# A fused decoder layer whose engines follow written-out step lists: every list laid out anew

## The chip, the core and the metric

The kernel runs on one core of a Trainium2 chip. Its five instruction queues are named as in the profile: PE (TensorE, matrix products), DVE (VectorE), ACT (ScalarE), POOL (GpSimd) and SP (SyncE, which here only issues the transfers). Each queue runs its instructions strictly in the order in which they are written and talks to the others through semaphores. The metric is the device time of one execution in microseconds (us).

## What is computed

One decoder layer over x of shape (8, 256, 512): a linear attention with a memory, a gated long convolution (32 heads of 8 rows each, along the 512 columns), and a feed-forward block with 4-bit weights. Each is followed by a residual sum and a layer norm.

```python
x = layernorm(x + attn(x, w_q, w_k, w_v, w_o, gate, M, z))
#   attn: sq, sk = elu(q)+1, elu(k)+1; memory = sq@M/(sq@z); local = causal sums of sk,v; mix by sigmoid(gate); @ w_o
x = layernorm(x + conv(ctx, ctx, x, ssm_kernel, D, head_dim=8))
#   kv = k_i * v_j per head; y = causal convolution of kv with ssm_kernel (+ D on lag 0); out_j = sum_i y_ij * q_i
x = layernorm(x + ffn(x))
#   gate, up = x @ dequant(gate_up).T; h = silu(gate)*up; y = h @ dequant(down).T; y / rms(y)
```

## The kernel before

The work has two parts. The **first stage** prepares weights and runs the attention of all tokens in eight slots (i = 0 to 7). The **bodies** then run eight groups of 256 rows. Body g computes the convolution of group g and, one group behind, the feed-forward block of group f = g - 1. Body 1 is mixed into the end of the first stage (its steps carry a "+" in the START lists). Body 2 is written out, bodies 3 to 6 are a hardware loop, body 7 is written out without the work that would prepare a ninth group, and body 8 (the LAST lists) holds only the feed-forward block of the last group.

What sets the order on each engine is a list of step names, written by hand into `decoder_layer`: START_SYNC, START_PE, START_DVE, START_ACT and START_POOL for the first stage and body 1, PE_ORDER, DVE_ORDER, ACT_ORDER and POOL_ORDER for a body, and the LAST lists. The helper `run` walks each list. A step is a fixed handful of instructions with its own waits. No scheduler comes after that.

The steps of a body that the text below names:

- PE: `g{i}_{p}` is one quarter (p = 0 to 3) of the gate-and-up product of hidden tile i (0 to 10), four products of 256 columns (L1284, L1286) into one of three PSUM banks (i modulo 3). `y0_{i}` and `y1_{i}` are the down product of tile i for row half 0 or 1, three products of 512 columns (L1297 to L1299). y1 runs a body late. `c{u}` is convolution unit u (0 to 15), three products of 288 columns for each of u%4+1 blocks (L137 to L139), `d0`, `d1` are c0, c1 of the next group. `ct`, `rt`, `xt` are four transposes each (L102).
- ACT: `rs{i}_{p}` rescales bank i between two quarters (two instructions, L1134). `gu{i}` is the silu (L1141), `hh{i}` rounds the hidden tile to 16 bits (L1151), `hk{h}` and `kn` round the key-value products (L180), `n0`, `n1` square the output rows (L1162). `rv`, `ct`, `xt`, `ho` are copies.
- DVE: `gu{i}` multiplies gate and up (L1201), `tm{u}` multiplies convolution unit u with the queries (five instructions, L239 to L257), `lk{h}` and `ln` make the low half of the key-value products (L216), `a`, `b`, `e` finish the output rows (L1207 to L1232), `bs`, `bn`, `nm` the norm behind the convolution, `kq` turns the queries.
- POOL: `pr{h}` and `pn` make the key-value products (four instructions, L197 to L208), `tr{h}` adds up the terms of four units (L297, L299, L304), `hl{i}` makes the low half of hidden tile i (L1102), `a`, `b`, `bn` are roots of a single column (L1098, L308).

The waits that matter: `g{i}_{p}` waits for `rs{i}_{p}`. `g{i}_0` waits for the DVE's `gu{i-3}`, and g0_0 also for both `xt` steps of the body before. `c{u}` waits for `tm{u-2}`, and from one h = u//4 to the next for `lk`. DVE `gu{i}` waits for ACT `gu{i}` and for `hh{i-2}` and `hl{i-2}`, since the tile buffer `h32` has two places. `pr{h}` waits for the `lk` before it, `hk{h}` for `pr{h}`, `lk{h}` for `hk{h}`. `tr{h}` waits for `tm{4h+3}`. `rt1` waits for `tr3`. `y0_{i}` and `y1_{i}` wait for `hl{i}`.

In the first stage the names are: Q and V (projections of a slot), X (its transposes), S, M, N, T, O (scores, memory, local sums, transposed output, out projection), `nm{i}` on ACT (the normalized rows of slot i), and on SP `x{i}` (load of slot i into a ring of five buffers), `st{i}` (its nine stores: rows once, blocks of 64 KB eight times), `xq`, `xr`, `cx`, `toe` (loads for the convolution) and `tw` (the split kernel to memory). `xq0` waits until the blocks of slots 0 to 3 have landed.

## Time and profile before

| | us |
|---|---|
| median of 3 runs | 537.16 |
| lowest and highest | 536.99, 537.49 |
| the profiled execution: its span | 535.3 |
| PE busy in it | 508.7 (95%) |
| ACT, POOL, DVE busy in it | 415.7, 394.7, 374.4 |
| DMA queue, share of 16 engines | 29.6% |

The span runs from the first to the last instruction that the profiler saw. The timed figure lies 1.9 us above it. In the profile a product that follows another overlaps it, because its end is modelled. How long a product really holds PE is therefore read from the distance of two starts. An engine's step is written here as name@time, with the time from the start of the body on PE, that is from the first product of y1_0.

### The profile page before, as it was taken

The numbers are of one execution on the slowest core, as the hardware profiler recorded it, in microseconds if no ns is written. First come the engines' busy times: TensorE is split into PE (matmuls) and PEld (weight loads), VectorE is DVE, ScalarE is ACT, GpSimd is POOL, SyncE is SP. The second block draws the span as 40 slices with busy tenths as digits, with TensorE's granted clock in tenths as the row PEclk, the third lists the DMA queues.
The fourth block names the chain that finished last, engine by engine and source line by source line (L and its number), as shares of the span: only waits on it lengthen the run. The fifth ranks groups of instructions, "written<-read, shape, count | busy, mean of one in ns | idle before, by whom it ended". The sixth has DMA issues, their size and how long they took to land.

```text
span 535.3 us, 11768 instructions
## 1 busy us (share of the span) xinstructions
PE 508.7 (95%) x3676; PEld 377.6 (71%) x3676; DVE 374.4 (70%) x1145; ACT 415.7 (78%) x994; POOL 394.7 (74%) x449
## 2 busy tenths in 40 slices
...
GB/s 224 203 39 63 169 142 180 128 80 99 87 112 24 159 127 86 23 100 79 60 1 117 59 59 0 118 59 59 13 130 14 39 33 49 0 1 42 1 21 39
DMA packets 66146, 40.63 MB, mean 76 GB/s; under 512 B 37882, under 2 KB 55418, under 8 KB 66106
## 3 DMA queue, kind: packets, MB, share of 16 engines
q1 hardware_dynamic: 66106, 40.13, 29.6%
...
q14 instruction: 20, 0.16, 0.1%
...
## 4 chain that ended last, share of the span: by engine, by line
PE 36%; POOL 27%; issue 19%; ACT 5%; DVE 4%; SPq 4%; DMA 2%; POOLq 1%; DVEq 0%; ACTq 0%
POOL shared L297 9%; POOL h_lo L1102 5%; SPq L415 4%; POOL kv L197 3%; PE p_cv L137 3%; PE p_cv L139 3%; PE p_cv L138 3%; PE p_n L1299 3%; PE p_n L1297 3%; PE p_n L1298 3%; POOL shared L299 2%; PE p_x L1284 2%; PE p_x L1286 2%; PE p_qk L1284 2%; PE p_qk L1286 2%
## 5 line engine op out<-in xcount | busy, mean ns | idle before, releaser
L1102 POOL TENSOR_TENSOR h_lo<-w,h_hi 128x256 f16<-128x256 f32 x88 | 73.6, 842 | 44.6 <-ACT h_hi L1151 43.0
L137 PE MATMUL p_cv<-kv_hi,toe 128*128 128x288 f16 x320 | 91.6, 286 | 1.3 <-DVE shared L257 1.3
L139 PE MATMUL p_cv<-kv_hi,toe 128*128 128x288 f16 x320 | 91.5, 286 | 0.0
L138 PE MATMUL p_cv<-kv_lo,toe 128*128 128x288 f16 x320 | 91.5, 286 | 0.0
L1134 ACT ACTIVATE p_qk<-p_qk,rescale 128x256 f32<-128x256 f32 x192 | 78.3, 451 | 12.5 <-PE p_qk L1286 11.9
L297 POOL TENSOR_TENSOR shared<-shared 128x1024 f32<-128x1024 f32 x32 | 76.8, 2399 | 8.9 <-DVE shared L257 8.8
L1134 ACT ACTIVATE p_x<-p_x,rescale 128x256 f32<-128x256 f32 x192 | 78.4, 452 | 6.2 <-PE p_x L1286 6.0
L1134 ACT ACTIVATE p_s<-p_s,rescale 128x256 f32<-128x256 f32 x144 | 59.0, 456 | 11.2 <-PE p_s L1286 11.1
L1297 PE MATMUL p_n<-wd_hi,h_hi 128*128 128x512 f16 x176 | 66.8, 379 | 0.0
L1298 PE MATMUL p_n<-wd_lo,h_hi 128*128 128x512 f16 x176 | 66.7, 379 | 0.0
L1299 PE MATMUL p_n<-wd_hi,h_lo 128*128 128x512 f16 x176 | 66.7, 379 | 0.0
L1284 PE MATMUL p_qk<-x_hi,wg_hi 128*128 128x256 f16 x256 | 63.0, 273 | 3.6 <-DVE x_lo L285 2.1
L1284 PE MATMUL p_x<-x_hi,wg_hi 128*128 128x256 f16 x256 | 62.9, 273 | 0.7 <-ACT p_x L1134 0.2
L1286 PE MATMUL p_x<-x_lo,wg_hi 128*128 128x256 f16 x256 | 62.8, 273 | 0.0
L1286 PE MATMUL p_qk<-x_lo,wg_hi 128*128 128x256 f16 x256 | 62.8, 273 | 0.0
L239 DVE TENSOR_TENSOR shared<-p_cv,qv 128x128 f32<-128x128 f32 x128 | 36.1, 282 | 32.4 <-PE p_cv L139 31.8
L216 DVE TENSOR_TENSOR kv_lo<-kv,kv_hi 128x1152 f16<-128x1152 f32 x32 | 52.6, 1642 | 3.4 <-ACT kv_hi L180 3.4
L242 DVE TENSOR_TENSOR shared<-p_cv,qv 128x128 f32<-128x128 f32 x128 | 49.7, 388 | 0.0
L299 POOL TENSOR_TENSOR shared<-shared 128x512 f32<-128x512 f32 x32 | 47.7, 1492 | 2.5
L1284 PE MATMUL p_s<-x_hi,wg_hi 128*128 128x256 f16 x192 | 47.1, 273 | 0.9 <-ACT p_s L1134 0.9
L1286 PE MATMUL p_s<-x_lo,wg_hi 128*128 128x256 f16 x192 | 47.1, 273 | 0.0
L180 ACT CAST kv_hi<-kv 128x1152 f16<-128x1152 f32 x32 | 37.3, 1166 | 10.9 <-POOL kv L208 7.2
...
## 6 DMA issues: line engine op xcount, KB each, us to landing
...
```

The costliest lines, as they stand in the source:

```text
L137: nc.tensor.matmul(dst, hi, kh, start=(mb == 0), stop=False)
L138: nc.tensor.matmul(dst, hi, kl, start=False, stop=False)
L139: done = nc.tensor.matmul(dst, lo, kh, start=False, stop=(mb == lb))
L297: nc.gpsimd.tensor_tensor(T[:, :, 0:256], T[:, :, 0:256], T[:, :, 256:512], ALU.add).then_inc(cv.tree, 1)
L299: nc.gpsimd.tensor_tensor(T[:, :, 0:128], T[:, :, 0:128], T[:, :, 128:256], ALU.add).then_inc(cv.tree, 1)
L1102: nc.gpsimd.tensor_tensor(h_lo[:, i, :], h32[:, i % 2, :], h_hi[:, i, :], ALU.subtract).then_inc(h_low, 1)
L1134: done = nc.scalar.activation(sums, sums, ACT.Copy, scale=rescale[:, p - 1, part * GI + i:part * GI + i + 1])
L1284: nc.tensor.matmul(dst, whi, cv.x2_hi[:, k, :], start=(k == 0 and part == 0), stop=False, skip_group_check=True)
L1286: done = nc.tensor.matmul(dst, whi, cv.x2_lo[:, k, :], start=False, stop=True, skip_group_check=True)
L1297: nc.tensor.matmul(p_y[t][:], h_hi[:, i, c], wd_hi[:, i, :], start=(i == 0), stop=False)
L1298: nc.tensor.matmul(p_y[t][:], h_hi[:, i, c], wd_lo[:, i, :], start=False, stop=False)
L1299: done = nc.tensor.matmul(p_y[t][:], h_lo[:, i, c], wd_hi[:, i, :], start=False, stop=(i == GI - 1))
```

## The change

Every list is replaced by another permutation of the same steps. Within each body (first stage with body 1, full body, last body) the set of steps on each engine is the same as before. Two waits are added: `deviations` waits for the semaphore that its own engine raised in the slot before, and `add_residual` waits for `fin_made` of the group before, which its own engine raised, too.

```diff
         def deviations(i):
             act.wait_ge(mean_made, i + 1)
+            wait(act, deviated, 2 * i)
...
         def add_residual(f, t):
             dve.wait_ge(rr_made[t], f + 1)
             dve.wait_ge(cv.x2_held[t], f + 1)
+            wait(dve, fin_made[t], f)
...
-    START_SYNC = ("x3 x4 cx2 st0 cx3 tw0 x5 st1 st2 x6 st3 toe0 xq0 xq2 toe1 xq1 x7 cx5 cx4 xr1 xr0 toe2 st4 cx6 xq3 "
+    START_SYNC = ("cx2 tw0 toe0 x3 cx3 x4 st0 x5 st1 x6 st2 st3 xq0 xq1 x7 xq2 toe1 cx4 xr0 cx5 xq4 toe2 cx6 "
...
-    PE_ORDER = ("y1_0 g0_0 g1_0 y1_1 g0_1 y1_2 ct0 g1_1 g0_2 y1_3 y1_4 g2_0 g0_3 c2 g1_2 g3_0 c3 y1_5 g2_1 g1_3 g3_1 "
+    PE_ORDER = ("y1_0 y1_1 g0_0 g1_0 g2_0 y1_2 y1_3 g0_1 g1_1 y1_4 g2_1 g0_2 y1_5 g1_2 ct0 g2_2 c2 c3 c4 "
+                "g0_3 g1_3 g2_3 c5 g3_0 g4_0 y1_6 y1_7 g3_1 g4_1 g5_0 y1_8 g3_2 c6 c7 c8 g5_1 g4_2 y1_9 g3_3 "
+                "c9 c10 g4_3 g5_2 y1_10 g6_0 g7_0 g5_3 c11 g6_1 g8_0 g7_1 c12 c13 g6_2 g7_2 c14 c15 ct1 g6_3 "
...
-    DVE_ORDER = ("tm0 tm1 gu0 lk1 tm2 tm3 gu1 tm4 tm5 gu2 lk2 tm6 tm7 tm8 gu3 tm9 tm10 lk3 tm11 gu4 a1 tm12 gu5 tm13 "
+    DVE_ORDER = ("tm0 tm1 lk1 tm2 tm3 gu0 gu1 gu2 tm4 lk2 tm5 tm6 tm7 tm8 tm9 gu3 gu4 lk3 gu5 tm10 tm11 a1 "
...
-    POOL_ORDER = ("pr1 hl0 pr2 tr0 hl1 pr3 tr1 hl2 hl3 pn a1 hl4 hl5 tr2 tr3 hl6 bn0 b1 hl7 bn1 hl8 hl9 hl10 a0 b0").split()
+    POOL_ORDER = ("pr1 pr2 hl0 hl1 tr0 pr3 hl2 tr1 hl3 pn tr2 hl4 hl5 a1 tr3 b1 bn0 hl6 bn1 hl7 hl8 hl9 hl10 "
+                  "a0 b0").split()
...
-    LAST_DVE = ("gu0 gu1 gu2 a1 gu3 gu4 gu5 b1 gu6 gu7 gu8 e1 gu9 gu10 A1 B1 a0 b0 E1 e0").split()
+    LAST_DVE = "gu0 gu1 gu2 gu3 gu4 a1 b1 gu5 gu6 gu7 gu8 gu9 gu10 e1 A1 B1 a0 E1 b0 e0".split()
```

**POOL, in a body, from the end of pr3 on** (rows of body 7, which has no pn; `shared<-shared` in a row of three is one `tr`, `h_lo` is one `hl`). Before:

```order
L208 TENSOR_TENSOR kv32<-kT1 128x128
L297 TENSOR_TENSOR shared<-shared 128x4x256
L299 TENSOR_TENSOR shared<-shared 128x4x128
L304 TENSOR_TENSOR shared<-shared 128x32x8
L1102 TENSOR_TENSOR h_lo<-w32,h_hi 128x256 x2
L1098 TENSOR_TENSOR rr<-ms,halfneg 128x1
L1102 TENSOR_TENSOR h_lo<-w32,h_hi 128x256 x2
L297 TENSOR_TENSOR shared<-shared 128x4x256
```

After:

```order
L208 TENSOR_TENSOR kv32<-kT1 128x128
L1103 TENSOR_TENSOR h_lo<-w32,h_hi 128x256
L297 TENSOR_TENSOR shared<-shared 128x4x256
L299 TENSOR_TENSOR shared<-shared 128x4x128
L304 TENSOR_TENSOR shared<-shared 128x32x8
L1103 TENSOR_TENSOR h_lo<-w32,h_hi 128x256
L297 TENSOR_TENSOR shared<-shared 128x4x256
```

hl2 moved ahead of tr1, and hl1 (not in these rows) ahead of tr0; hl3 stays right behind tr1, and in a full body pn and tr2 follow it, with hl4 and hl5 behind tr2 and not ahead of it.

**DVE, in a body, around lk3** (rows of body 2; `kv_lo1<-kv32,kv_hi1` is lk3, `w32<-` is a `gu`, a run of five `shared<-p_cv` is a `tm`). Before:

```order
L216 TENSOR_TENSOR kv_lo1<-kv32,kv_hi1 128x1152
L239 TENSOR_TENSOR shared<-p_cv1,qv1 128x32x4
L242 TENSOR_TENSOR shared<-p_cv1,qv1 128x4x8x4
L248 TENSOR_TENSOR shared<-p_cv1,qv1 128x32x2
L251 TENSOR_TENSOR shared<-p_cv1,qv1 128x2x16x2
L257 TENSOR_TENSOR shared<-p_cv1,qv1 128x2x2x32
L1201 SCALAR_TENSOR_TENSOR w32<-p_x,c_up,w32 128x256
L1207 TENSOR_SCALAR ms<-ss 128x1
```

After:

```order
L1202 SCALAR_TENSOR_TENSOR w32<-p_qk,c_up,w32 128x256
L1202 SCALAR_TENSOR_TENSOR w32<-p_x,c_up,w32 128x256
L216 TENSOR_TENSOR kv_lo1<-kv32,kv_hi1 128x1152
L1202 SCALAR_TENSOR_TENSOR w32<-p_s,c_up,w32 128x256
L239 TENSOR_TENSOR shared<-p_cv0,qv1 128x32x4
L242 TENSOR_TENSOR shared<-p_cv0,qv1 128x4x8x4
L248 TENSOR_TENSOR shared<-p_cv0,qv1 128x32x2
L251 TENSOR_TENSOR shared<-p_cv0,qv1 128x2x16x2
L257 TENSOR_TENSOR shared<-p_cv0,qv1 128x2x2x32
```

Before, tm10 stood ahead of lk3 and tm11, gu4 behind it; now gu3, gu4, lk3 and gu5 stand in a row, and tm10 and tm11 come behind gu5.

**SP, in the first stage, after the first fifteen loads.** Before:

```order
L406 DMA z<-in_x 128x2x512
L406 DMA fin<-in_x 128x2x512
L419 DMA cnat<-in_ctx 128x1x512
L410 DMA x_rows<-ring 128x2x512
L415 DMA x_blocks<-ring 8x64x32 x8
L419 DMA cnat<-in_ctx 128x1x512
L462 DMA toeplitz_rows<-kpad 32x1280
L406 DMA ring<-in_x 128x2x512
L410 DMA x_rows<-ring 128x2x512
L415 DMA x_blocks<-ring 8x64x32 x8
```

After:

```order
L419 DMA cnat<-in_ctx 128x1x512
L462 DMA toeplitz_rows<-kpad 32x1280
L423 DMA toe<-toeplitz_rows 128x4x512
L406 DMA z<-in_x 128x2x512
L419 DMA cnat<-in_ctx 128x1x512
L406 DMA fin<-in_x 128x2x512
L410 DMA x_rows<-ring 128x2x512
L415 DMA x_blocks<-ring 8x64x32 x8
L406 DMA ring<-in_x 128x2x512
L410 DMA x_rows<-ring 128x2x512
```

The load of slot 5 (`ring<-in_x`) now stands directly behind the stores of slot 0, whose buffer it reuses; the loads of slots 3 and 4 (`z`, `fin`) stand behind three other transfers.

## Rows read from the trace of the kernel before

**Rows 1.** Busy time by stretch: bounds, length, PE, PEld, DVE, ACT, POOL (instructions), PE clock, DMA.

```profile
1.28:127.30 126.02, 115.16 (x744) 92.41 (x744) 92.86 (x266) 79.22 (x163) 88.76 (x119) 1.00 0.59 140
...
176.10:226.93 50.83, 50.83 (x388) 37.90 (x386) 37.51 (x120) 42.20 (x105) 43.05 (x45) 1.00 0.44 97
...
278.14:329.34 51.20, 51.02 (x387) 37.71 (x386) 38.47 (x121) 42.89 (x106) 42.90 (x45) 1.00 0.22 61
431.74:481.92 50.18, 49.57 (x370) 35.65 (x369) 35.17 (x118) 39.92 (x101) 39.70 (x41) 1.00 0.08 22
481.92:525.20 43.28, 41.91 (x276) 26.07 (x274) 12.45 (x28) 36.18 (x98) 10.08 (x16) 1.00 0.07 19
```

**Rows 2.** Timeline of PE around a body's start: start, duration, line, operands [idle before].

```profile
329.12 0.38 PE L1299 MATMUL p_n<-wd_hi,h_lo 128*128 128x512 f16 x1
329.34 0.38 PE L1297 MATMUL p_n<-wd_hi,h_hi 128*128 128x512 f16 x1
...
330.33 0.28 PE L1284 MATMUL p_qk<-x_hi,wg_hi 128*128 128x256 f16 x1 [0.18 <-DVE x_lo L285]
330.45 0.27 PE L1286 MATMUL p_qk<-x_lo,wg_hi 128*128 128x256 f16 x1
330.56 0.27 PE L1284 MATMUL p_qk<-x_hi,wg_hi 128*128 128x256 f16 x1
...
336.43 0.30 PE L137 MATMUL p_cv<-kv_hi,toe 128*128 128x288 f16 x1
336.56 0.29 PE L138 MATMUL p_cv<-kv_lo,toe 128*128 128x288 f16 x1
```

**Rows 3.** Timeline of POOL, tr0 to hl2 of the body that starts at 278.14.

```profile
291.59 2.37 POOL L297 TENSOR_TENSOR shared<-shared 128x1024 f32<-128x1024 f32 x1
...
295.48 1.64 POOL L304 TENSOR_TENSOR shared<-shared 128x256 f32<-128x256 f32 x1 [0.16 <-POOL shared L299]
297.08 0.67 POOL L1102 TENSOR_TENSOR h_lo<-w,h_hi 128x256 f16<-128x256 f32 x1
297.71 1.27 POOL L197 TENSOR_TENSOR kv<-kT 128x512 f32<-128x512 f32 x1
...
300.44 2.36 POOL L297 TENSOR_TENSOR shared<-shared 128x1024 f32<-128x1024 f32 x1
...
304.92 2.41 POOL L1102 TENSOR_TENSOR h_lo<-w,h_hi 128x256 f16<-128x256 f32 x2
```

**Rows 4.** Timeline of DVE: three of the 32 instructions of L216 (`lk`, `kl`).

```profile
287.00 1.36 DVE L216 TENSOR_TENSOR kv_lo<-kv,kv_hi 128x1152 f16<-128x1152 f32 x1 [0.58 <-ACT kv_hi L180]
...
294.81 1.72 DVE L216 TENSOR_TENSOR kv_lo<-kv,kv_hi 128x1152 f16<-128x1152 f32 x1
...
93.52 2.81 DVE L216 TENSOR_TENSOR kv_lo<-kv,kv_hi 128x1152 f16<-128x1152 f32 x1
```

**Rows 5.** Timeline of POOL and ACT at a body's end: a0, b0, pr1, an rs.

```profile
330.49 0.55 POOL L1098 TENSOR_TENSOR rr<-ms,halfneg 128x1 f32<-128x1 f32 x1 [2.16 <-DVE ms L1207]
...
333.96 1.27 POOL L197 TENSOR_TENSOR kv<-kT 128x512 f32<-128x512 f32 x1
...
330.98 0.81 ACT L1134 ACTIVATE p_qk<-p_qk,rescale 128x256 f32<-128x256 f32 x2 [0.25 <-PE p_qk L1286]
```

**Rows 6.** Costliest groups: counts, busy us, mean ns of one, idle before by releaser.

```profile
L180 ACT CAST kv_hi<-kv 128x1152 f16<-128x1152 f32 x32 | 37.3, 1166 | 10.9 <-POOL kv L208 7.2 <-PE p_cv L139 3.7
...
L1151 ACT CAST h_hi<-w 128x256 f16<-128x256 f32 x88 | 36.1, 411 | 2.2 <-DVE w L1201 1.8
...
L1201 DVE SCALAR_TENSOR_TENSOR w<-p_x,c_up,w 128x256 f32<-128x256 f32 x32 | 15.4, 481 | 14.3 <-ACT w L1141 14.3
```

**Rows 7.** SP's queue in the first stage: the block stores of slot 0, the first `xq` loads.

```profile
38.37 7.19 SPq L415 DMA_DIRECT2D x_blocks<-ring x8
...
83.34 4.90 SPq L426 DMA_DIRECT2D xq<-x_blocks x2
```

**Rows 8.** Timeline of PE at the start of the last body: g0_1 after its wait.

```profile
485.88 0.28 PE L1284 MATMUL p_qk<-x_hi,wg_hi 128*128 128x256 f16 x1 [0.55 <-ACT p_qk L1134]
```

More of the change, by code:

```diff
@@ L1359, in decoder_layer @@
-    START_ACT = ("xa0 kw0 kw1 xb0 kw2 kw3 re0 ge0 vk0 ks0 xa1 xb1 lc0 rv0 wh0 wh1 re1 ok0 kt0 wh2 rv1 wh3 qs0 xa2 vk1 "
[8 rows of a table removed]
-                 "+hh10 nm7 +xt1 +n0").split()
-    START_POOL = ("id0 ms0 ws0 ws1 ws2 ws3 ws4 ws5 pr0 ws6 ws7 pw0 ws8 ws9 ws10 pr1 ws11 ws12 ws13 ws14 ws15 pw1 ws16 "
-                  "pw2 ws17 ws18 ws19 ws20 ws21 ws22 ws23 pw3 ws24 ws25 ws26 ws27 ws28 ws29 ws30 ws31 ws32 pr2 pw4 tr0 "
-                  "pr3 tr1 pr4 tr2 tr3 pq0 +pr1 pq1 +pr2 pw5 +tr0 +hl0 +hl1 pw6 +pr3 +hl2 +tr1 +hl3 +pn +hl4 +tr2 +hl5 "
-                  "+hl6 +tr3 +hl7 +bn0 pw7 +hl8 +bn1 +hl9 +hl10 +a0 +b0").split()
@@ L1374, in decoder_layer @@
-    PE_ORDER = ("y1_0 g0_0 g1_0 y1_1 g0_1 y1_2 ct0 g1_1 g0_2 y1_3 y1_4 g2_0 g0_3 c2 g1_2 g3_0 c3 y1_5 g2_1 g1_3 g3_1 "
[3 rows of a table removed]
-                "y0_8 y0_9 xt1 y0_10").split()
-    DVE_ORDER = ("tm0 tm1 gu0 lk1 tm2 tm3 gu1 tm4 tm5 gu2 lk2 tm6 tm7 tm8 gu3 tm9 tm10 lk3 tm11 gu4 a1 tm12 gu5 tm13 "
-                 "kq0 tm14 tm15 b1 gu6 gu7 ln kq1 bs0 bn0 bs1 bn1 gu8 nm0 gu9 nm1 gu10 xt0 xt1 a0 b0 e1 e0").split()
-    ACT_ORDER = ("rv0 rs0_1 rs1_1 rs0_2 tl rs0_3 rs1_2 gu0 hk1 hh0 rs1_3 rs2_1 rs3_1 rs2_2 gu1 rs3_2 rs2_3 hk2 gu2 hh1 "
-                 "ct0 rs4_1 rv1 rs3_3 rs5_1 rs4_2 rs5_2 gu3 hh2 hk3 rs4_3 rs5_3 rs6_1 n1 hh3 gu4 rs6_2 ho0 gu5 hh4 "
-                 "rs7_1 hh5 kn rs6_3 rs7_2 rs8_1 ct1 rs7_3 rs8_2 gu6 gu7 rs8_3 hh6 rs9_1 rs10_1 rs9_2 ho1 rs10_2 rs9_3 "
-                 "hh7 gu8 rs10_3 gu9 hh8 gu10 hh9 xt0 hh10 xt1 n0").split()
```

39 lines of the change are left out of this document (25 added, 14 removed), and 54 rows, old and new, of tables (LAST_PE, PE_ORDER, START_ACT, START_DVE).

## The prediction

> **What bounds the kernel now.** I read the busy times by stretch first, then the timeline of PE at the stretches' edges, then POOL's and DVE's timelines inside one body. In the body at 176.10 PE is busy for all of its 50.83 us, and in the looped bodies for all but 0.18 of 51.20 [rows 1]. Distances of starts tell what a product really costs: 0.216 us at 512 columns (329.12 to 329.34), 0.11 at 256, 0.12 to 0.13 at 288 [rows 2]. So a `y` takes 0.65 us of PE, a `g` 0.44, a `c` of k blocks 0.37 k, four transposes 0.44. With these a full body holds 50.7 us of PE work: 22 y 14.2, 44 g 19.2, the convolution 14.7, 24 transposes 2.6. The looped bodies give away 0.4 to 0.5 us, nearly all of it in one place: y1_0 starts at 329.34 and would be done at 329.99, but g0_0 starts at 330.33, released by DVE's x_lo [rows 2]. Nothing can be won in a body beyond that half microsecond, and everything can be lost. Slack is elsewhere: the stretch 1.28 to 127.30 has 126.0 us of which PE is busy 115.2, and the last body has waits such as the 0.55 us at g0_1 [rows 1, 8]. POOL is the second bound: busy 42.9 of 51.2 us in a looped body [rows 1], in an order in which each piece waits for DVE or ACT in between.
>
> **What POOL's pieces cost.** A `pr` holds POOL for 2.73 us (297.71 to 300.44), an undisturbed `tr` for 4.48 (300.44 to 304.92). The `tr0` of the same body took 5.49 (291.59 to 297.08), with its L304 at 1.64 us [rows 3], and in that time DVE's lk2 ran, 294.81 to 296.53, in 1.72 us where lk1 took 1.36 [rows 4]. A `kl` that met the 2.37 us instruction L297 took 2.81 [rows 4]. So a `lk` and a POOL step that meet cost POOL about 1.0 us, and the `lk` waits for the end of POOL's instruction. The Trainium skill states this in "SBUF — State Buffer", section "Who interferes with whom": a vector instruction with two SBUF inputs and a GpSimd instruction that reads SBUF exclude one another for the whole instruction. By that rule each meeting would cost POOL up to the whole 1.36 us of the `lk`, where these rows show 1.0.
>
> **The body, walked through in the new order.** PE positions are sums of the step costs above.
> - The tail first. In the loop now the last product of y0_10 ends at 329.50 and pr1 starts at 333.96, 4.5 us later, through n0, a0 (POOL at 330.49), b0 on DVE and b0 on POOL [rows 2, 5]. In the new PE order d1 stands behind y0_10, so y0_10 ends 0.6 us before the next body starts and pr1 starts at 3.9 (now 4.6).
> - pr1 ends at 6.8. ACT must first do rs0_1, rs1_1, rs2_1, rs0_2, rv0, rs1_2, rs2_2 (0.73 us each for a pair [rows 5], 0.5 for rv0), the last fed by g2_1@5.4, so hk1 (1.17 us [rows 6]) runs 7.2 to 8.4, lk1 8.4 to 9.8, pr2 9.9 to 12.6. There is no hl0 in between to fill POOL's 3 us.
> - g0_3 stands behind 6 y, 9 g, ct0, c2, c3 and c4, at 11.2 (now 6.3 by the same count). The three silus and two products behind it (0.48 us each [rows 6]) let hh0 end at 13.6, hl0 runs 13.7 to 14.35, hl1 to 15.0, tr0 starts at 15.0 (now 13.45, as 291.59 less 278.14 [rows 1, 3]).
> - lk2 can start at 16.5 (pr2, then two rs, then hk2), but L297 of tr0 holds until 17.3: lk2 ends at 18.6, tm5 at 19.6. PE stands at c7@18.9, which waits for tm5. **Stall 1: 0.8 us.**
> - tr0 pays the meeting and ends at 20.5, pr3 at 23.2, hl2 at 23.8, tr1 starts. On DVE gu3, gu4 and lk3 stand in a row and gu4 needs g4_3@24.5, so lk3 falls on 26.5 to 28.9, within tr1, which then ends at 29.3; hl3 at 30.0. DVE's gu5 needs hl3 and ends at 30.5. PE has g8_0 behind 11 y, 27 g, ct0 and c2 to c11, at 29.25 plus stall 1, 30.05, and it needs gu5. **Stall 2: 0.6 us.**
> - Behind gu5 DVE has tm10 and tm11, done at 32.2. c13 would start at 31.8 and needs tm11. **Stall 3: 0.5 us.**
> - POOL goes on without a pause: pn to 32.7, tr2 to 37.2, hl4, hl5, a1 to 39.0, tr3 to 43.4. rt1 stands at 41.85 plus 1.9, 43.75: no further stall. gu7 (needs hl5) ends at 39.3, g10_0 stands at 39.4: none.
> - At the end DVE's ln stands behind gu10, at 49.6 to 51.0, and meets hl9. y0_9 stands at 50.2 and needs hl9, which ends at 50.3 without the meeting and 51.1 with it; d0 needs ln. **Stall 4: between 0.1 and 0.9**, taken at 0.3, since which of the two comes first hangs on 0.1 us.
> - In return g0_0 now has y0_8, y0_9, d0, y0_10, d1, y1_0 and y1_1 between it and xt1, and its wait goes.
>
> Sum: 50.7 + 0.8 + 0.6 + 0.5 + 0.3 = 52.9, with 0.1 for handovers 53.0, against 51.2. That is 1.8 us for each of bodies 3 to 6 and 2.1 for body 2: **9.3 us**. The bounds: below, no stall at all, 50.8 and a gain of 0.4 a body; above, stall 4 in full and a second meeting at 1.36, 54.0 and a loss of 2.8.
>
> **Body 7** has no pn, but stalls 1 to 3 stand ahead of it: 48.8 of PE work plus 1.9, 50.7 against 50.18 [rows 1]: **0.5 us**.
>
> **The last body** holds 40.5 us of PE work in 43.3 [rows 1]. The new lists drop ho0 from ACT's start (it goes to the end, behind n0, beside a0 and its root) and ask g0, g1, g2 in turn, in the order in which ACT serves them. Walking it the same way I find waits of 0.2 at g2_2, 0.1 at g3_2, 0.1 at g3_3, 0.2 at g7_2 and some of 0.1, 0.8 in all, so 41.4 where 43.3 stand. Behind the last product, B1's root comes ahead of a0's, and E1 leaves b0's root alone: 0.2 less. Together with 0.2 for the first g0_0, which has three y ahead of it: **minus 2.3 us**, bounds 0 and minus 3.
>
> **The first stage and body 1.** Moved: on SP, the transfer of the kernel and toe0 ahead of x3 and x4, x5 directly behind st0 and x6 behind st1; on ACT nm0 behind qs1, xa3, vk2 and xb3; on DVE u2 and u3 ahead of steps of slots 1 and 2, sk0 and fs0 exchanged. x3 lands at 31 or so and Xa3 needs it at 36: free. nm0 ends at 44 (now 37.9), so st0's nine issues (7.2 us [rows 7]) end at 52, x5 waits 3 us for their landing, x6 likewise, and st3's last block lands 2 us later than now, where xq0 leaves at 83.34 [rows 7]. From there to rt1 POOL runs tr0, pr3, tr1, pr4, tr2, tr3 in both orders, so 2 us come out late. They are given back: pq1 now stands ahead of body 1's pr1 (2.73 us), and c1 and c2 (1.8 us) stand between xt0 and g0_0 as filling. On PE g0_0 has 1.1 us more work ahead of it and comes at 128.7 where it came at 127.3 [rows 1], so 0.3 net. Body 1 is no better or worse by a count that I trust. **Plus 0.4 us**, bounds minus 2 and plus 3.
>
> **The two added waits** ask for what their own engine has finished a slot or a body earlier, nothing is queued by them: 0.
>
> Total: 0.4 + 9.3 + 0.5 - 2.3 = +7.9 us. The profiled span of 535.3 becomes 543.2; the median lies 1.9 above the span, so **545.0 us**.
>
> **The rivals.**
> 1. *The loop runs clean, and the kernel is faster.* Stalls 1 to 3 hang on one run of POOL from 3.9 to 30.0. If it were 1.0 us shorter (lk3 ahead of or behind tr1, or hk1 earlier), gu5 would be done at 29.5 and stalls 2 and 3 vanish; at 1.5 us also stall 1. For it: PE's content is no more than before and the order asks banks in turn. Against it: DVE's gu3, gu4, lk3 in a row put lk3 into tr1. All clean is 5 times minus 0.4, minus 1.5 in body 7 and minus 2.3, with plus 0.4: 532, with small waits left 533. Chance 0.20.
> 2. *Only one stall of the loop is there*, 0.5 to 0.8 a body: 538 to 541. Chance 0.17.
> 3. *More than I count.* Every meeting of a `lk` costs its full 1.36, and stall 4 is full: 0.35 twice and 0.6, 1.2 a body more, 551. By the Trainium skill's page "SBUF — State Buffer" the first half of that is the rule. Chance 0.12.
> 4. *The order does nothing that can be told from no change* (0.2%, about what a measurement of this kernel resolves), by the first stage giving what the loop takes. Chance 0.05.
> The forecast, 541 to 548, keeps 0.46.
>
> **How the numbers follow.** The range reaches from the middle between rivals 1 and 2 to most of rival 3: 535 to 550, leaving 0.15 below and 0.05 above. Faster: rival 1 and a little of the rest, 0.22. Same 0.06, slower 0.72.
>
> **What would show it.** Starts of y1_0 53.0 us apart in the loop (clean: 50.8). Idle PE before c7 (released by L257), g8_0 (by L1202) and c13 (by L257). tr0 and tr1 near 5.5 us both. No idle before g0_0. tr0 at 94.5 to 95 in the first stage. It would be wrong above all if hl3 is done before 29 us into the body, or if PE idles in the loop somewhere that this walk does not name.

## The result, and the profile after

| | before | after |
|---|---|---|
| median (4 runs each) | 537.33 | 548.99 |
| lowest and highest | 536.99, 537.98 | 548.24, 549.54 |
| span of the profiled execution | 535.3 | 547.6 |
| chain that ended last: PE, POOL | 36%, 27% | 23%, 37% |

The change makes the kernel slower: ratio 1.0218, 95% interval 1.0204 to 1.0233. The forecast was 545.0 in a range of 535 to 550. The span grew by 12.3 us. The starts of the bodies (the first product of y1_0, in the last body the first product of its list) say where:

| stretch | forecast | measured |
|---|---|---|
| first stage and body 1 (start of body 2 at 176.10, now 179.14) | +0.4 | +3.0 |
| bodies 2 to 6 (255.6 us, now 267.4) | +9.3 | +11.7 |
| body 7 (50.18, now 50.73) | +0.5 | +0.55 |
| last body to the end of the span (53.4, now 50.3) | -2.3 | -3.0 |

Busy time by stretch, with the columns of [rows 1]. The second line is body 2, the third a looped body, then body 7 and the last body with its tail (43.28 us in [rows 1] leaves the tail out).

```profile
1.28:131.94 130.66, 118.53 (x752) 94.24 (x752) 95.21 (x269) 76.90 (x160) 89.09 (x119) 1.00 0.54 134
179.14:232.53 53.39, 51.75 (x387) 37.45 (x386) 39.55 (x123) 44.69 (x110) 42.10 (x45) 1.00 0.53 124
286.02:339.53 53.51, 51.48 (x388) 37.48 (x386) 38.97 (x121) 42.69 (x107) 41.96 (x45) 1.00 0.20 59
446.52:497.25 50.73, 49.43 (x371) 35.82 (x369) 36.48 (x119) 39.08 (x100) 38.37 (x41) 1.00 0.08 22
497.25:547.59 50.34, 40.92 (x276) 26.13 (x274) 15.08 (x36) 36.67 (x99) 11.91 (x19) 0.95 0.11 27
```

The granted clock is 1.00, the full level of 2.4 GHz, in all of them but the last. There it is 1.00 as well up to PE's last product at 538.3, and 0.72 on average in the 9.3 us behind it, in which PE has nothing to do. PE's busy time includes the ends that the profile models, so 2.03 us of idle in the looped body stand for 2.8 us lost, as the distances of starts give it (50.7 us of work in 53.5).

The timeline of PE in that body, around its four waits (c7, g8_0, c13, d0). Line numbers are one or two higher than in the rows of before: a product of g is L1286 or L1288, y is L1299 to L1301.

```profile
304.80 0.29 PE L139 MATMUL p_cv<-kv_hi,toe 128*128 128x288 f16 x1
305.53 0.30 PE L137 MATMUL p_cv<-kv_hi,toe 128*128 128x288 f16 x1 [0.45 <-DVE shared L257]
...
315.80 0.27 PE L1288 MATMUL p_qk<-x_lo,wg_hi 128*128 128x256 f16 x1
316.78 0.28 PE L1286 MATMUL p_s<-x_hi,wg_hi 128*128 128x256 f16 x1 [0.71 <-DVE w L1202]
...
317.91 0.29 PE L139 MATMUL p_cv<-kv_hi,toe 128*128 128x288 f16 x1
318.51 0.30 PE L137 MATMUL p_cv<-kv_hi,toe 128*128 128x288 f16 x1 [0.31 <-DVE shared L257]
...
336.83 0.38 PE L1301 MATMUL p_n<-wd_hi,h_lo 128*128 128x512 f16 x1
337.77 0.29 PE L137 MATMUL p_cv<-kv_hi,toe 128*128 128x288 f16 x1 [0.56 <-DVE kv_lo L216]
```

Take the distance of the two starts and subtract what the first product holds PE: 0.73 less 0.12 is 0.61 before c7. In the same way 0.87 before g8_0, 0.48 before c13, 0.72 before d0. The idle before g0_0 in [rows 2] is gone. DVE in that body: lk2, then lk3 and what stands behind it, then ln (answers [rows 4], where an undisturbed one took 1.36).

```profile
302.55 2.06 DVE L216 TENSOR_TENSOR kv_lo<-kv,kv_hi 128x1152 f16<-128x1152 f32 x1 [0.62 <-ACT kv_hi L180]
...
312.72 2.18 DVE L216 TENSOR_TENSOR kv_lo<-kv,kv_hi 128x1152 f16<-128x1152 f32 x1
316.24 0.48 DVE L1202 SCALAR_TENSOR_TENSOR w<-p_s,c_up,w 128x256 f32<-128x256 f32 x1 [1.34 <-POOL h_lo L1103]
...
335.74 1.81 DVE L216 TENSOR_TENSOR kv_lo<-kv,kv_hi 128x1152 f16<-128x1152 f32 x1
```

POOL in the same body, tr0, then hl2, tr1 and hl3, then hl9 and hl10 (answers [rows 3]).

```profile
301.03 2.36 POOL L297 TENSOR_TENSOR shared<-shared 128x1024 f32<-128x1024 f32 x1
303.47 2.27 POOL L299 TENSOR_TENSOR shared<-shared 128x512 f32<-128x512 f32 x1
305.90 0.73 POOL L304 TENSOR_TENSOR shared<-shared 128x256 f32<-128x256 f32 x1 [0.16 <-POOL shared L299]
...
309.32 0.68 POOL L1103 TENSOR_TENSOR h_lo<-w,h_hi 128x256 f16<-128x256 f32 x1
309.95 2.38 POOL L297 TENSOR_TENSOR shared<-shared 128x1024 f32<-128x1024 f32 x1
312.41 1.27 POOL L299 TENSOR_TENSOR shared<-shared 128x512 f32<-128x512 f32 x1
313.76 1.72 POOL L304 TENSOR_TENSOR shared<-shared 128x256 f32<-128x256 f32 x1
315.44 0.67 POOL L1103 TENSOR_TENSOR h_lo<-w,h_hi 128x256 f16<-128x256 f32 x1
...
335.66 2.41 POOL L1103 TENSOR_TENSOR h_lo<-w,h_hi 128x256 f16<-128x256 f32 x2 [0.45 <-ACT h_hi L1152]
```

Here the exclusion can be read off. lk2 was issued at 302.55, while L297 ran until 303.39. It ended at 304.61, 1.2 us behind the end of L297. L299 took 2.27 where an undisturbed one takes 1.27, and it ended 1.1 us behind lk2. So first DVE waits for POOL's instruction, then POOL's next one for DVE's. Both pay: lk2 took 0.70 us more than its undisturbed 1.36, L299 1.0 more. tr0 (301.03 to 306.63) and tr1 (309.95 to 315.48) both take 5.5 to 5.6 us. hl3 follows tr1 and ends at 316.11, and DVE's gu5 starts 0.13 us later, DVE having been idle for 1.34 us. g8_0 follows gu5. That is the chain of stall 2.

In the first stage the transfers on SP, as far as the prediction speaks of them (answers [rows 7]): the blocks of slot 0, the first xq, then what was not foreseen, xr2 at 118.23 with xr1 behind it.

```profile
46.02 6.15 SPq L415 DMA_DIRECT2D x_blocks<-ring  x8
...
86.89 0.96 SPq L426 DMA_DIRECT2D xq<-x_blocks  x2
...
118.23 1.35 SPq L430 DMA_DIRECT2D xr<-x_rows  x2
```

And on DVE, bq1 of the first stage, which adds the rows that xr1 loads:

```profile
125.05 0.69 DVE L265 TENSOR_TENSOR shared<-p_ct,xr 128x512 f32<-128x512 f32 x1 [1.98 <-DMA xr<-x_rows]
```

### The profile page after: what moved, and what is told of

Same layout as the page of the kernel before. It is cut to its first block, busy times and chain, and to the rows that moved or that the text cites. A ratio compares the mean times of both kernels' runs of the same rounds, so it can differ in the third digit from the quotient of the medians.

```text
span 547.6 us, 11783 instructions
## 1 busy us (share of the span) xinstructions
PE 512.4 (94%) x3676; PEld 377.4 (69%) x3676; DVE 375.1 (69%) x1145; ACT 413.5 (76%) x994; POOL 388.6 (71%) x449
## 4 chain that ended last, share of the span: by engine, by line
POOL 37%; PE 23%; issue 18%; DVE 11%; ACT 4%; DMA 3%; SPq 3%; POOLq 1%; DVEq 0%; ACTq 0%
POOL shared L297 10%; POOL h_lo L1103 7%; POOL shared L299 4%; POOL kv L197 4%; PE p_n L1299 2%; PE p_n L1301 2%; PE p_n L1300 2%; POOL kv L207 2%; POOL kv L202 2%; SPq L415 2%; POOL shared L304 2%; PE p_qk L1286 2%; PE p_x L1288 2%; PE p_qk L1288 2%; PE p_x L1286 2%
## 5 line engine op out<-in xcount | busy, mean ns | idle before, releaser
L1103 POOL TENSOR_TENSOR h_lo<-w,h_hi 128x256 f16<-128x256 f32 x88 | 65.7, 756 | 38.0 <-ACT h_hi L1152 37.5
L1135 ACT ACTIVATE p_qk<-p_qk,rescale 128x256 f32<-128x256 f32 x192 | 79.7, 466 | 16.0 <-PE p_qk L1288 15.7
L297 POOL TENSOR_TENSOR shared<-shared 128x1024 f32<-128x1024 f32 x32 | 76.7, 2396 | 13.5 <-DVE shared L257 13.5
L1135 ACT ACTIVATE p_x<-p_x,rescale 128x256 f32<-128x256 f32 x192 | 80.1, 473 | 2.5 <-PE p_x L1288 2.5
L1299 PE MATMUL p_n<-wd_hi,h_hi 128*128 128x512 f16 x176 | 66.8, 379 | 0.1
L1301 PE MATMUL p_n<-wd_hi,h_lo 128*128 128x512 f16 x176 | 66.7, 379 | 0.0
L1286 PE MATMUL p_qk<-x_hi,wg_hi 128*128 128x256 f16 x256 | 62.9, 273 | 1.2 <-DVE w L1202 1.0
L216 DVE TENSOR_TENSOR kv_lo<-kv,kv_hi 128x1152 f16<-128x1152 f32 x32 | 56.9, 1779 | 9.2 <-ACT kv_hi L180 9.2
L1286 PE MATMUL p_x<-x_hi,wg_hi 128*128 128x256 f16 x256 | 62.9, 273 | 0.0
L1288 PE MATMUL p_x<-x_lo,wg_hi 128*128 128x256 f16 x256 | 62.8, 273 | 0.0
L1288 PE MATMUL p_qk<-x_lo,wg_hi 128*128 128x256 f16 x256 | 62.8, 273 | 0.0
L197 POOL TENSOR_TENSOR kv<-kT 128x512 f32<-128x512 f32 x32 | 41.1, 1284 | 23.8 <-DVE kv_lo L216 23.7
L1286 PE MATMUL p_s<-x_hi,wg_hi 128*128 128x256 f16 x192 | 47.2, 273 | 4.1 <-DVE w L1202 4.0
L299 POOL TENSOR_TENSOR shared<-shared 128x512 f32<-128x512 f32 x32 | 48.8, 1524 | 2.5
L137 PEld LDWEIGHTS p_cv<-kv_hi,toe 128*128 128x128 f16 x320 | 31.2, 98 | 24.3 <-DVE shared L257 10.2
```

What stands on the lines that cost most here:

```text
L137: nc.tensor.matmul(dst, hi, kh, start=(mb == 0), stop=False)
L297: nc.gpsimd.tensor_tensor(T[:, :, 0:256], T[:, :, 0:256], T[:, :, 256:512], ALU.add).then_inc(cv.tree, 1)
L299: nc.gpsimd.tensor_tensor(T[:, :, 0:128], T[:, :, 0:128], T[:, :, 128:256], ALU.add).then_inc(cv.tree, 1)
L1103: nc.gpsimd.tensor_tensor(h_lo[:, i, :], h32[:, i % 2, :], h_hi[:, i, :], ALU.subtract).then_inc(h_low, 1)
L1135: done = nc.scalar.activation(sums, sums, ACT.Copy, scale=rescale[:, p - 1, part * GI + i:part * GI + i + 1])
L1286: nc.tensor.matmul(dst, whi, cv.x2_hi[:, k, :], start=(k == 0 and part == 0), stop=False, skip_group_check=True)
```

## Experiments

All experiments have the two added waits. "The whole" is the median, a body's length the distance of y1_0's starts in the profiled execution. With the old first stage, the start of body 2 lay between 175.7 and 176.8 in eight kernels that share it, the one before among them, mostly because the wait before c2, behind xq0's landing, varies from 0.5 to 1.3 us. So parts of a microsecond in the whole are read from the bodies, where the looped ones of one kernel agree within 0.04 us.

### One part of the change at a time

**Full body only.**

```diff
 START_*, LAST_*                  (old lists)
-PE_ORDER, DVE_ORDER, ACT_ORDER, POOL_ORDER   (old)
+PE_ORDER, DVE_ORDER, ACT_ORDER, POOL_ORDER   (new)
```

> Only the four full-body lists are the new ones; the first stage, body 1 and the last body keep the old ones (537.3 us as a whole). Theory (the loss is in the body's own cycle: c7 behind tm5, g8_0 behind gu5, c13 behind tm11, d0 behind ln): bodies 2 to 6 cost the 11.7 us that they cost in the changed kernel and body 7 0.6, so 549.5 us, looped body 53.5 us. Rival (the stalls are handed on by the new first stage, whose steps leave POOL and DVE late): with the old first stage the looped body falls back towards 51.2 and the whole to 538 to 543.

Measured 549.67 (ratio 1.0233, 1.0216 to 1.0251). The looped body takes 53.50 and bodies 2 to 6 take 267.38 us, to 0.01 us what they take in the changed kernel. The four waits are the same in place, and in size to 0.01 us. So the loss of the loop is the body's own and nothing is handed on to it.

**First stage and body 1 only.** The new START lists, the other lists old.

> Only the first stage and body 1 are new. Theory (parts add up, the stretch up to body 2 is 3.0 us longer in the changed kernel): 540.3 us. Rival (what the new first stage leaves behind fits only the new body): body 2 also loses 1 to 2 us more, so 541 to 543. Rival (the old body takes the late start up in its own slack): below 539.

Measured 541.41 (1.0080, 1.0063 to 1.0096), so the first rival. Body 2 starts at 178.90, and it takes 52.24 us where it took 50.83. The timeline of ACT and then of PE at the start of body 2:

```profile
179.10 0.60 ACT L1163 ACTIVATE sq<-p_n 128x512 f32<-128x512 f32 x1
179.59 0.19 ACT L1163 ACTIVATION_READ_ACCUMULATOR sq<-p_n 128x1 f32 x1
179.68 1.51 ACT L632 ACTIVATE ring<-ring,shift,rs 128x512 f32<-128x512 f32 x2
181.09 0.60 ACT L174 COPY crev<-cnat 128x512 f32<-128x512 f32 x1
181.60 0.81 ACT L1135 ACTIVATE p_qk<-p_qk,rescale 128x256 f32<-128x256 f32 x2
```

```profile
181.22 0.38 PE L1301 MATMUL p_n<-wd_hi,h_lo 128*128 128x512 f16 x1
182.46 0.28 PE L1286 MATMUL p_qk<-x_hi,wg_hi 128*128 128x256 f16 x1 [0.86 <-ACT p_qk L1135]
```

The new ACT list ends with nm7 (L632, 1.51 us) behind n0. The old body asks rs0_1 for g0_1 behind one y, so g0_1 waits 1.02 us. The new body has y1_2 and y1_3 in between and hides nm7. Here start and body fit one another in the new lists, and testing one alone shows 1.4 us more loss than it causes in the changed kernel.

**Last body only.** The new LAST lists, the others old.

> Only the last body is new. Theory (its own order takes away the 3.1 us in which PE waited between the last bodies' products): 3.0 us less than before, 534.3 us. Rival (the gain came from how the new full body ends, with its hidden tiles and its norm done earlier, not from the last body's list): 536.5 to 537.5 us.

Measured 535.13 (0.9963, 0.9949 to 0.9977). By its own list the last body falls from 53.4 to 50.38 us, as in the changed kernel. But body 7 grows from 50.18 to 51.10, since the new last list begins with g0_0, which comes before the old body's xt1 is through ACT and DVE:

```profile
481.75 0.38 PE L1301 MATMUL p_n<-wd_hi,h_lo 128*128 128x512 f16 x1
482.89 0.28 PE L1286 MATMUL p_qk<-x_hi,wg_hi 128*128 128x256 f16 x1 [0.76 <-DVE x_lo L285]
```

The 3.0 us are the last body's own and 0.9 go at the seam. It is the fastest kernel that still computes everything.

### What makes the waits in the loop

All of these start from the kernel with the new full body only (549.67, looped body 53.50).

**One term step into DVE's idle time.**

```diff
-DVE_ORDER = "... gu3 gu4 lk3 gu5 tm10 tm11 a1 ..."
+DVE_ORDER = "... gu3 gu4 lk3 tm10 gu5 tm11 a1 ..."
```

> The new full body in the old surroundings (looped body 53.5 us, 549.7 as a whole), with one move on DVE: tm10 stands ahead of gu5, where DVE waited 28.88 to 30.23 for hl3, and not behind it. gu5 keeps its time (30.2), tm11 ends 0.8 us earlier, so the 0.48 before c13 goes. Theory A (POOL's run from hl0 to tr3, without a gap from 13.8 to 43.6, is a second bound just behind PE, with rt1 at 43.87 right behind tr3): rt1 now waits 0.2 to 0.4, and the looped body gains 0.1 to 0.3 only, so 548.2 to 549.2. Theory B (each wait of PE counts by itself): the looped body falls by 0.48 to 53.0, the whole by 2.4 to 547.3.

Measured 547.98 (1.0200, 1.0185 to 1.0216), the looped body 53.41. The 0.48 before c13 is gone and gu5 keeps its time (312.52, at 30.22 of the body). But PE now waits 0.19 before g10_0 (for gu7, which waits for hl5) and 0.1 before rt1, and every step of POOL from hl0@13.76 to tr3@43.59 stands where it stood, to 0.03 us. The body gains 0.09, a fifth of the wait that went. That is theory A for the loop. Of the 2.0 us of the span, 0.5 are bodies 2 to 6, 0.5 body 7, where the gain is not taken back (no pn), and 1.0 lies ahead of body 2, in the part that is the same code, so only half of the 2.0 us is an effect of the move.

**ln somewhere else.**

```diff
-DVE_ORDER = "... gu7 b1 bs0 ... gu9 gu10 ln xt1 ..."
+DVE_ORDER = "... gu7 b1 ln bs0 ... gu9 gu10 xt1 ..."
```

> The new full body in the old surroundings (549.7 us), with ln moved on DVE from behind gu10 to behind b1, into the idle 41.2 to 42.7. There it falls into tr3 of POOL (39.05 to 43.57), in place of hl10. Theory A (POOL's tr grows by 1.0 when it meets a low half of the key-value products, as tr0 and tr1 do with 5.5 against 4.5): tr3 ends 0.5 to 1.0 later and rt1 waits as much; hl10 falls from 1.74 to 0.67 and the 0.74 before d0 goes; looped body 53.3 to 53.8, the whole 548.7 to 551. Theory B (the length of tr depends on other things, and only the place of ln counts): rt1 doesn't wait, looped body 52.8, the whole 546.

Measured 550.53 (1.0245, 1.0229 to 1.0261), the looped body 53.67: theory A. The wait before d0 is gone and hl10 falls from 1.74 to 0.68 us. tr3 grows from 4.52 to 5.53, in its L299 as before, and rt1 waits for it by 0.85 us. POOL's tr3 and PE's rt1 behind it:

```profile
322.98 2.35 POOL L297 TENSOR_TENSOR shared<-shared 128x1024 f32<-128x1024 f32 x1
325.41 2.29 POOL L299 TENSOR_TENSOR shared<-shared 128x512 f32<-128x512 f32 x1
327.77 0.73 POOL L304 TENSOR_TENSOR shared<-shared 128x256 f32<-128x256 f32 x1
```

```profile
328.63 0.65 PE L102 MATMUL p_ct<-ident,shared 128*128 128x128 f32 x4 [0.68 <-POOL shared L304]
```

**The low halves cut to a ninth.**

```diff
+        w = slice(0, 9) if isinstance(g, int) and g < 2 else slice(0, 1)
-        nc.vector.tensor_tensor(cv.kv_lo[h % 2][:], cv.kv32[:], cv.kv_hi[h % 2][:], ALU.subtract)
+        nc.vector.tensor_tensor(cv.kv_lo[h % 2][:, w], cv.kv32[:, w], cv.kv_hi[h % 2][:, w], ALU.subtract)
```

> The new full body in the old surroundings (549.7 us); from body 2 on the steps lk and ln make only the first ninth of the low half (128 of 1152 columns), the rest of it keeps older values, so that work is left out. Theory A (the meetings of lk with tr on DVE and POOL carry all four waits): tr0 and tr1 fall from 5.5 to 4.5, hl10 from 1.7 to 0.7, all four waits go, looped body 50.7 to 51.0, the whole 535.5 to 537. Theory B (the order alone makes them: hl3 stands behind tr1, gu5 behind hl3, tm11 behind gu5): only the waits before c7 and d0 go, 0.87 and 0.48 stay, looped body 52.1, the whole 542.5.

Measured 534.16 (0.9941, 0.9926 to 0.9956), 1.3 us below the range of theory A, which left out that body 7 has three of the waits, too (bodies 7 and 8 take 1.9 us less together). All four waits are gone, the looped body takes 50.79 us, which is PE's own work, and PE has 76% of the chain that ended last. tr0 takes 4.61, tr1 4.51, hl10 0.67 us. It does not say yet whether the meetings did it or the time that DVE saved. A looped body of this kernel:

```profile
278.29:329.07 50.78, 50.78 (x388) 37.88 (x386) 34.59 (x121) 42.56 (x107) 38.95 (x45) 1.00 0.22 62
```

**The time kept, the second input taken away.** The same cut, and in its place a reduction over the other 1024 columns, which reads one buffer.

```diff
+            nc.vector.tensor_reduce(cv.spare[:], cv.kv32[:, 1:9]..., axis=X, op=ALU.add)
         nc.vector.tensor_tensor(cv.kv_lo[h % 2][:, w], cv.kv32[:, w], cv.kv_hi[h % 2][:, w], ALU.subtract)
```

> The new full body in the old surroundings (549.7 us, looped body 53.5). From body 2 on lk and ln make only the first ninth of the low half, and a sum over the other 1024 columns of the same buffer (one input from SBUF, its result is never read) fills up their time on DVE to about the 1.36 us of before; so the rest of the low half keeps older values. Theory A (what stretches POOL is that lk reads two inputs from SBUF, as the Trainium skill has it in SBUF - State Buffer, section Who interferes with whom, where a reduction never contends; by the rows alone the same is expected, since DVE's other steps beside a tr leave it at 4.5): tr0, tr1 at 4.5 to 4.6, hl10 at 0.7, no wait before g8_0 and c13, at most 0.1 before c7 and 0.3 before d0, looped body 50.8 to 51.3, the whole 534 to 537. Theory B (the waits come from DVE's 1.4 us at these places, whatever it does in them): tr0 and tr1 at 5.5 or the waits at c7 and d0 as before, looped body 52 or more, the whole above 541.

Measured 541.03 (1.0071, 1.0054 to 1.0088), the looped body 52.05, so neither. tr0 and tr1 are at 4.61 and 4.52 and the waits before g8_0 and c13 are gone, as theory A has it. d0 waits 0.34, as it has it. But c7 waits 0.90 and not 0.1. The two steps of lk2 on DVE, and POOL's tr0 beside them (L304 is here what L297 is elsewhere, L306 is L299):

```profile
296.52 1.22 DVE L221 TENSOR_REDUCE spare<-kv 128x1 f32<-128x1024 f32 x1 [0.62 <-ACT kv_hi L181]
297.65 1.21 DVE L223 TENSOR_TENSOR kv_lo<-kv,kv_hi 128x128 f16<-128x128 f32 x1
```

```profile
295.00 2.37 POOL L304 TENSOR_TENSOR shared<-shared 128x1024 f32<-128x1024 f32 x1
297.45 1.28 POOL L306 TENSOR_TENSOR shared<-shared 128x512 f32<-128x512 f32 x1
```

The reduction ran for 0.85 us beside POOL's L304, and that took its undisturbed 2.37. The little subtraction behind it, with its two inputs, needed 1.21 us for 128 columns (0.43 in lk3 of the same body): it waited until L306 was through at 298.73 and ended at 298.86. So the reduction disturbs nobody, and the remaining two-input piece was shut out for one more POOL instruction, which made lk2 end at 18.9 of the body and not at 18.6. What follows: the waits before g8_0 and c13 come from the two-input meeting, since DVE was almost as busy as before (38.2 us in a looped body, 39.0 without the cut), only with another kind of instruction. The wait before c7 is not separated by this run; in the cut one lk2 ended at 17.53, just behind L297, and c7 did not wait. By the rows of the changed kernel the meeting is enough to explain it: lk2 took 0.70 us longer than undisturbed, and c7 waited 0.61. That is worked out and not shown by a run. Before d0 0.34 of 0.72 us are left without a meeting.

### The first stage

Of these, all four take the new first stage with the old full and last body.

**The order of two loads.**

```diff
-START_SYNC = "... xr0 cx5 xq4 toe2 cx6 xr2 xr1 toe3 ..."
+START_SYNC = "... xr0 cx5 xq4 toe2 cx6 xr1 xr2 toe3 ..."
```

> As the kernel with only the new first stage, but on SP the load xr1 stands ahead of xr2, no longer behind it. xr2 loads group 1's rows into the buffer that bq0 of group 0 empties, so whatever stands behind it is issued only after bq0; in the changed kernel xr1 was issued at 118.23 and bq1 of DVE started at 125.05, behind its landing. Theory (this one place carries 2 of the 3 us of the first stage): bq1 starts about 2 us earlier and the whole is 1.5 to 2.5 us below the kernel with only the new first stage. Rival (the stores and the later norm of slot 0 set it, and bq1's wait is hidden by the next one): within 0.5 us of it.

Measured 539.43 (1.0045, 1.0028 to 1.0062), 2.0 us below the kernel without the swap, and body 2 starts at 176.92 where it started at 178.90. bq1 starts at 122.90, without a wait for rows, and not at 125.05. xr2 waits for bq0 to empty its buffer, and xr1, which had nothing left to wait for, stood behind it.

```profile
122.90 0.68 DVE L265 TENSOR_TENSOR shared<-p_ct,xr 128x512 f32<-128x512 f32 x1
```

**The norms of slots 6 and 7.** nm7 ahead of xt1 of body 1, nm6 behind hh7, pw6 ahead of hl6, nb6 behind gu7, all of body 1; with the swap above.

> The new first stage with xr1 ahead of xr2, old full and last body (539.4 us), and nm6 and nm7 (two squares of slots 6 and 7, 1.5 us each on ACT) moved: nm7 from the very end of ACT's start list, behind n0, to ahead of xt1 of body 1, nm6 from there to behind hh7, with its inputs pw6 and nb6 drawn ahead. Theory (in body 2 rs0_1 stands behind nm7, which ran 177.71 to 179.22, so g0_1 waits 1.03 us; the new full body hid that behind y1_2 and y1_3): body 2 falls from 52.23 to 50.8 to 51.2, the whole to 538.0 to 538.4. Rival (the norms only move the wait into body 1, to g9_0 or xt1, since ACT has no 1.5 us free there): body 1 longer by what body 2 gains, 539.0 to 539.8.

Measured 544.71 (1.0142, 1.0125 to 1.0159). Body 2 takes 51.37, so 0.87 of its 1.4 us were indeed nm7's, but body 1 lost 6 us, far beyond the rival. nm6 now stands ahead of rs8_1, it waits for nb6, that for pw6, and that stands on POOL behind tr3 until 167.25. ACT, and PE's g8_1:

```profile
168.63 1.52 ACT L632 ACTIVATE ring<-ring,shift,rs 128x512 f32<-128x512 f32 x2 [3.53 <-DVE shift L790]
170.06 0.78 ACT L1135 ACTIVATE p_s<-p_s,rescale 128x256 f32<-128x256 f32 x2
```

```profile
170.90 0.28 PE L1286 MATMUL p_s<-x_hi,wg_hi 128*128 128x256 f16 x1 [4.22 <-ACT p_s L1135]
```

**fs0 early.** In addition fs0 on DVE behind dn0.

> As the kernel with the moved norms, and fs0 on DVE (six small instructions on the scales) back behind dn0, where the old list had it near 18 us, from behind o2, where it ran 46.6 to 51.2 because its one-input instructions of 11 and 88 columns took 1.4 to 2.5 us beside POOL's unpacking copies, and where ra2 and rb2 stood behind it (1.46 us wait of PE before V3, st2 and all stores behind it late). Theory A (the delay of slot 2 goes on through nm2 and st2 to xq0 and so to c2): the wait before V3 goes, st2 and xq0 leave 1 to 2 us earlier, the whole falls by 1 to 2 us. Theory B (PE's gain is eaten at c2, whose wait is for xq0, and xq0 hangs on the loads x5 and x6 that stand between the stores): V3's wait goes, c2's wait grows by the same 1.5, within 0.4 us of the kernel with the moved norms.

Measured 546.80 (545.74 to 547.83; 1.0172, 1.0151 to 1.0192). It says nothing on the question: fs0 and sk0 stood in front of o0 and held it from 18.6 to 23.1 us, ACT's ok0 waited 5.05 us, and everything came 3 us later up to body 2.

**fs0 late.** Only the swap of the loads, and fs0 behind o3.

> The new first stage with xr1 ahead of xr2, old full and last body (539.4 us), and fs0 on DVE behind o3, where DVE stood idle from 59.2 to 63.0 us, not behind o2, where it held DVE from 46.0 to 50.6 with ra2 and rb2 queued behind it. (Behind dn0, as in the run before, it waited at 18.6 to 22 in front of o0 and pushed everything 3 us back, which answered nothing.) Theory A (the delay of slot 2 goes on by nm2 and st2, issued at 69.0, to the loads xq0 at 86.25 and kq0 and so to c2): the wait of 1.46 before V3 goes, st2 and xq0 leave 1 to 2 us earlier, the whole comes to 537.4 to 538.4. Theory B (xq0 hangs on the loads x5 and x6 that stand between the stores, x6 issued at 66.09): V3's wait goes, st2 at most 0.5 earlier, c2's wait grows from 2.0 to 3 or more, the whole within 0.4 of 539.4.

Measured 539.68 (1.0050, 1.0033 to 1.0067), no gain over 539.43. fs0 takes 2.1 us there and not 4.5, and V3 starts 0.9 us earlier. But N3 now waits 1.36 us for DVE's AT (0.57 before the move) and starts at 56.66, 0.2 later than without it, and w23 waits another 0.7. st2 and xq0 leave at 69.84 and 87.08, not earlier than their 69.01 and 86.25. The whole is what theory B gave, but not by its way: the gain is gone five microseconds further on, long before xq0 and c2. So the 1.46 us before V3 were no loss that moving fs0 gives back.

### A faster kernel that did not come

The old full body gives away 0.35 us before g0_0, and the new last body 0.9 at the seam.

```diff
-PE_ORDER = "... xt0 y0_7 y0_8 y0_9 xt1 y0_10"
+PE_ORDER = "... xt0 y0_7 y0_8 xt1 y0_9 y0_10"
-LAST_PE = "g0_0 g1_0 g2_0 y1_0 g0_1 ..."
+LAST_PE = "y1_0 g0_0 g1_0 g2_0 g0_1 ..."
```

> The old first stage and full body with the new last body (535.1 us as a whole), and two moves on PE: in the full body xt1 stands one product earlier (ahead of y0_9, its input nm1 was made 1.3 us before it), and in the last body y1_0 stands ahead of g0_0. Theory (g0_0 waits for the last transposed rows by way of ACT and DVE, 0.35 in each looped body and 0.92 at the head of the last body): the looped body falls from 51.20 to 50.85, four or five times 0.35, and 0.9 goes from body 7 to 8, so 532.4 to 533.0. Rival (xt1 runs into the rounding on ACT or the bank and its chain does not move with it, or POOL's run holds rt1): 534 to 535, with a wait at rt1 or at xt1 in place of the one at g0_0.

Measured 537.85 (1.0012, 1.0003 to 1.0021), so the rival, and worse than it. xt1 wants the bank that DVE's x_lo of xt0 drains at 329.25:

```profile
329.40 0.63 PE L102 MATMUL p_ct<-ident,shared 128*128 128x128 f32 x4 [0.43 <-DVE x_lo L285]
```

The wait at g0_0 is gone, xt1 waits 0.59 and c2 0.36, and the looped body takes 51.77 in place of 51.21. At the seam 0.06 us were won: bodies 7 and 8 take 101.42 us together, where with the plain new last body they took 101.48.

## Why the prediction was right, point by point

**Sign and range: right**, but the range held by its width and not by the sum. The span grew by 12.3 us, where the sum had 7.9. At 548.99 the time lies above the 541 to 548 that the prediction called its forecast, 1.0 us below the upper end of a range that was drawn up to 550 for the sake of rival 3. Of the missing 4.4 us, 2.6 lie in the first stage with body 1 and 2.4 in bodies 2 to 6, and the last body gave back 0.7.

**The walk through the body: right in mechanism and place.** All four waits stand where it put them, before c7, g8_0, c13 and d0, with the releasers it named, and no fifth one. Up to tr3 its times held to 0.3 us or better: hl0 forecast 13.7 and measured 13.76, tr0's end 20.5 and 20.6, lk3's 28.9 and 28.88, hl3's 30.0 and 30.09, tr3's 43.4 and 43.57. Stalls 1 to 3 were given 1.9 us and measured 1.96, and here two misses cancel: stall 1 was given 0.8 and measured 0.61, stall 2 0.6 and 0.87, stall 3 0.5 and 0.48.

**Stall 4: under-sized.** The prediction saw a race of ln with hl9 and hl10, between 0.1 and 0.9, and took 0.3, for no better reason than that 0.1 us decides. It measured 0.72. ln was issued at 49.72 of the body, 0.08 us behind the start of hl9. So hl9 was not lengthened (49.64 to 50.31), ln waited for its end, took 1.81 us in place of 1.36 and ended at 51.53 where the walk had 51.0; hl10 behind it took 1.74 in place of 0.67. The walk had left out its own rule, that a `lk` waits for the end of POOL's instruction. Four looped bodies at 2.3 and body 2 at 2.6 are 11.7 us for a forecast of 9.3. This term is most of the difference there.

**The first stage: the step that failed.** Forecast +0.4, measured +3.0. What comes late was seen, but sized too small: st0's issues end at 52.17 (forecast 52) and x5 and x6 wait 2.8 us each (3), but xq0 leaves 3.55 us later than before and not 2, and POOL's tr0 2.6 us later (92.74 before, 95.35 now). What failed is the sentence that these microseconds are given back, since pq1 now stands ahead of pr1 with its 2.73 us. pq1 is the root for the norm of the rows that bq1 makes. First the kernel before, then the changed one:

```profile
123.38 0.56 POOL L308 TENSOR_TENSOR rs<-ve,halfneg 128x1 f32<-128x1 f32 x1 [0.53 <-DVE ve L275]
...
127.08 0.55 POOL L308 TENSOR_TENSOR rs<-ve,halfneg 128x1 f32<-128x1 f32 x1 [3.97 <-DVE ve L275]
```

Already before, with pr1 ahead of it, pq1 found POOL idle for 0.53 us and waited for DVE. pr1 cost it nothing, so there was nothing to give back. In the new order it waits for DVE again, 3.97 us, of which 2.2 come from bq1's wait for the rows of xr1, as the run with the two loads swapped shows. SP's queue behind the xq loads was not walked. One row of it, xr2 ahead of xr1, is worth 2.0 us of the stretch. With the swap pq1 starts at 124.92, still 1.5 us later than before, and the stretch is 0.8 us longer than before; where these 0.8 arise is open, and they are less than the 1.1 us by which the start of body 2 varies with the old first stage. g0_0 came at 131.94 and not at 128.7. Without the 1.1 us of work that was moved ahead of it, it is 3.5 us late where the prediction had 0.3, and body 1 made up 0.5 of them.

**Body 7** +0.55 for +0.5. **The last body** -3.0 for -2.3, the bound of the range that was given. It is the new list's own, since it comes out the same behind the old body 7.

**The rivals.** A clean loop is ruled out by the rows, and the run with the cut low halves shows that it would have cost 50.79 a body, as the 50.7 and 50.8 of the prediction. Its statement that stalls 2 and 3 hang on the run of POOL is borne out where the reduction takes the meeting away: both go, with DVE almost as busy. But the argument that a POOL run shorter by 1.0 us would do should have had a second sentence: if PE's waits are shortened without POOL, PE stands at rt1 instead. tm10's move took away 0.48 and gained 0.09. The third rival, 551, had two halves. The second, a full stall 4, came nearly true (0.72 of 0.9). The first, each meeting at the full 1.36 us, did not: the three meetings measured here cost POOL 1.0 (L299, 1.27 to 2.27), 1.0 (L304, 0.73 to 1.72) and 1.1 (hl10, 0.67 to 1.74). On the mechanism, the Trainium skill, "SBUF — State Buffer", section "Who interferes with whom", says that a vector instruction with two SBUF inputs contends with a GpSimd instruction that reads SBUF, and that a reduction does not. The rows agree with both: a meeting with lk2 lengthens L299, and the reduction leaves POOL's instruction at its 2.37. What a meeting costs POOL is decided by the measured 1.0 to 1.1, not by the 1.36 that the prediction derived from the rule.

**The two added waits: right at 0.** The kernel with the new last body alone has them in the old surroundings. Its body 2 starts at 176.11 and its looped body takes 51.21, where the kernel before has 176.10 and 51.20.
